# One order per engine, a transposed detour for the modulation, and gates folded into weights in a two-layer adaLN transformer

## What is computed

```python
x = L0_attn_x                                             # (8, 512, 128)
mod = (_silu(L0_c) @ L0_wmod).reshape(8, 6, 1, -1)
sa, ca, ga, sb, cb, gb = (mod[:, k] for k in range(6))
ga = (2 * (ga >= 0) - 1) * jnp.maximum(jnp.abs(ga), 0.25)  # gb the same
h = _layernorm(x) * (1 + ca) + sa
x = x + ga * _L0_attn_ref(h, ...)    # 16 query heads, 4 key heads of 64, rotary, 512 keys
h = _layernorm(x) * (1 + cb) + sb
x = x + gb * _L0_ffn_ref(h, ...)     # FP4-rounded activations and weights, 128 -> 352 -> 128
...                                   # layer 1: the same frame with its own c and wmod
x = x + ga * _L1_attn_ref(h, ...)    # 16 heads of 8; each token attends over the 8 sequences
h = _layernorm(x) * (1 + cb) + sb
x = x + gb * _L1_ffn_ref(h, ...)

def fp4_quant_dequant(x):            # blocks of 16 along the last dimension
    scale = jnp.maximum(jnp.max(jnp.abs(xb), axis=-1, keepdims=True) / 6.0, 1e-12)
    xn = xb / scale                  # |xn| goes to the nearest of 0 .5 1 1.5 2 3 4 6
    return (_GRID[jnp.searchsorted(_MID, jnp.abs(xn))] * jnp.sign(xn) * scale).reshape(shape)
```

## Time and profile before

| | |
|---|---|
| median of 3 runs | 1376.96 us (1372.1 to 1377.42) |
| the profiled execution, its own time | 1373.02 us |
| its span, first to last instruction | 1371.2 us |
| first part (layer 0's attention) | 0 to about 851 us |
| second part (what most of the diff touches) | about 851 to 1371 us |
| mean granted clock of TensorE | 0.899 |

### The profile page before, as it was taken

One profiled execution on the slowest core, in us unless ns is written; L12 is line 12 of the kernel. 1 busy time (PEld: TensorE's weight loads), 2 busy tenths in 40 slices (PEclk: granted clock), 3 DMA queues, 4 the chain that ended last, 5 costly groups with the idle time before them and its releaser, 6 DMA issues. The chain is left out here.

```text
span 1371.2 us, 29825 instructions
## 1 busy us (share of the span) xinstructions
PE 1128.8 (82%) x10832; PEld 711.5 (52%) x10832; DVE 1057.5 (77%) x1468; ACT 625.6 (46%) x1217; POOL 930.0 (68%) x808
## 2 busy tenths in 40 slices
PE   5889999989999989999999996586657776856865
PEld 2245565645655645655655655354335554545654
DVE  4588968868878768779789776677797777789895
ACT  2245645536546446455456452345444343423332
POOL 3379878768788768798798773333578686684331
PEclk9699999999999989999999997688868886887988
DMA  5112112112111111121121120000000000000000
GB/s 151 35 36 59 37 32 60 41 27 56 41 44 41 37 40 47 36 54 43 28 56 43 31 57 21 8 1 1 0 0 0 1 1 1 0 8 9 9 16 23
DMA packets 48627, 42.17 MB, mean 31 GB/s; under 512 B 7869, under 2 KB 46808, under 8 KB 48472
## 3 DMA queue, kind: packets, MB, share of 16 engines
q1 hardware_dynamic: 48040, 39.36, 11.6%
q10 hardware_dynamic: 432, 0.79, 0.2%
HBM read 6.42 MB, written 2.10 MB: 6 GB/s over the span
## 5 line engine op out<-in xcount | busy, mean ns | idle before, releaser
L509 ACT ACTIVATE a_probs<-a_ps_s 128x512 f32<-128x512 f32 x512 | 303.8, 596 | 326.6 <-PE a_ps_s L417 322.4
L742 POOL TENSOR_TENSOR a_p_lo<-a_probs 128x512 f16<-128x512 f32 x384 | 419.0, 1113 | 34.2 <-ACT a_probs L509 31.8
L670 DVE TENSOR_REDUCE a_nmx<-a_ps_m 128x2 f32<-128x1024 f32 x256 | 311.4, 1217 | 34.6 <-PE a_ps_m L400 33.9
L433 PE MATMUL a_ps_o<-a_v_hi,a_probs 128*128 128x65 f16 x2048 | 244.1, 196 | 15.4 <-DVE a_p_lo L677 7.9
L434 PE MATMUL a_ps_o<-a_v_lo,a_probs 128*128 128x64 f16 x2048 | 241.4, 194 | 0.0
L435 PE MATMUL a_ps_o<-a_v_hi,a_p_lo 128*128 128x65 f16 x2048 | 241.1, 195 | 0.0
L433 PEld LDWEIGHTS a_ps_o<-a_v_hi,a_probs 128*128 128x128 bf16 x2048 | 189.9, 99 | 87.9 <-issue 58.9
L415 PE MATMUL a_ps_s<-a_qq,a_kk 128*128 128x512 f16 x512 | 198.0, 387 | 8.2 <-issue 5.3
L434 PEld LDWEIGHTS a_ps_o<-a_v_lo,a_probs 128*128 128x128 bf16 x2048 | 191.8, 99 | 25.1 <-issue 1.5
L417 PE MATMUL a_ps_s<-a_qq,a_k_l 65*128 65x512 f16 x512 | 198.3, 387 | 0.0
L435 PEld LDWEIGHTS a_ps_o<-a_v_hi,a_p_lo 128*128 128x128 f16 x2048 | 191.5, 98 | 0.0
(11 more groups left out here) (234 smaller groups left out, 2108.7 us busy)
## 6 DMA issues: line engine op xcount, KB each, us to landing
a_qq<-a_rhi SPq DMA_DIRECT2D x128, 128.0 KB, 2.4
a_qq<-a_rlo SPq DMA_DIRECT2D x128, 64.0 KB, 2.1
a_kk<-a_rhi SPq DMA_DIRECT2D x64, 64.0 KB, 2.0
a_k_l<-a_rlo SPq DMA_DIRECT2D x32, 64.0 KB, 2.1
out_x<-x_sb SPq DMA_DIRECT2D x8, 256.0 KB, 2.3
a_qq<-a_nmT SPq DMA_DIRECT2D x64, 2.0 KB
a_probs<-in_wq ACTq DMA_DIRECT2D x1, 512.0 KB, 5.1
a_wo<-in_wo SPq DMA_DIRECT2D x1, 512.0 KB, 12.3
```

Of the source, the lines that this page charges most:

```text
L433: nc.tensor.matmul(out, hi, v_hi[:, b % 2, kt, g, 0:65], start=(kt == 0), stop=False)
L509: nc.scalar.activation(probs[:, p % 2, kt, h, :], ps_s[:, i % 2, :], ACT.Exp, scale=DH0 ** -0.5).then_inc(exp_done, 1)
L670: nc.vector.tensor_reduce(nmx[:, p % 2, i:2 * QT:QT], ps_m[:, n % 2, :, :], axis=X, op=ALU.max, negate=True).then_inc(free[n % 2], 1)
L742: nc.gpsimd.tensor_tensor(p_lo[:, p % 2, kt, h, :], pr, pr.bitcast(BF16)[:, 1:2 * L:2], ALU.subtract).then_inc(lo_pool, 1)
```

## The change

1. **Modulation by a detour (`HF`, `HB`).** `HS` no longer multiplies and adds on VectorE. TensorE turns the normalised input (`HF`, four transposes), ScalarE applies scale and shift as per-partition columns while it copies out of PSUM (four activations), TensorE turns it back (`HB`, four transposes), and `HS` reads the result from the PSUM bank, which it holds until it is done.
2. **Gates in weights.** For each FFN, GpSimd makes eight diagonal matrices of the gate (`PD`), and six products of 512 columns (`("P", "wd", f, k, half)`) give down weights for each sequence; two more (`"wo"`) do the same for the output weights. So `Y` is one addition. The output bias goes through the same diagonal matrices (`LY`: a full 128-row fp32 product in place of a 2-row fp16 one). The spread tables, `bc`, `PM8`, `PWO` and three of the four `G` go; `G` now spreads one gate.
3. **Denominator on TensorE (`DS`).** Eight products against the identity sum the probabilities, ScalarE copies, VectorE keeps the reciprocal.
4. **Head layout.** Query and key columns are stored channel-major, `(d h)` and no longer `(h d)`, so `SR` reads with a step of 16 elements.
5. **Order.** `merged_pipeline()` gives way to `merged_order(engine)`, with a table of offsets of its own for each engine and no extra `STEP` between groups 7 and 8.

```diff
-            nc.tensor.matmul(ps_s[0:B, 0, :], cT, wmod[:, 2 * D:6 * D], start=True, stop=True).then_inc(m8_full, 1)
+            nc.tensor.matmul(ps_s[0:B, 0, 0:D], cT, wmod[:, 2 * D:3 * D], start=True, stop=True).then_inc(m8_full, 1)
...
-        if -4 <= s < 0:
-            slots[7].append(("G", s + 4))
+        if s == -1:
+            slots[7].append(("G",))
...
+GROUP_AT = {
+    "PE": {"T1": -131, "GU": (-43, -19, 58, 93), "TD": (396, 407, 423, 426), "HF": -347, "HB": -250},
...
+                if kind == "HF":
+                    n = it[1]
+                    pe.wait_ge(xhat_ok, n + 1)
+                    for t in range(QT):
+                        last = nc.tensor.transpose(bank[:, t * 128:(t + 1) * 128], xhat[:, t, :], ident[:])
+                elif kind == "HB":
+                    n = it[1]
+                    pe.wait_ge(hT_ok, n + 1)
+                    for t in range(QT):
+                        last = nc.tensor.transpose(bank[:, t * 128:(t + 1) * 128], hT[:, t, :], ident[:])
...
+                elif kind == "DS":
+                    r = it[1]
+                    pe.wait_ge(prob_ok, r + 1)
+                    for j in range(B):
+                        last = nc.tensor.matmul(bank[:, 0:B * H1], ident[:], prob[:, :, j, :],
+                                                start=(j == 0), stop=(j == B - 1))
...
+                    elif it[1] == "wd":
+                        f, k, half = it[2:]
+                        pe.wait_ge(diag_ok, 2 * f + 1)
+                        k0, rows = K_TILES[k]
+                        last = nc.tensor.matmul(bank[0:rows, :], ffn_w[f][1][:, k0:k0 + rows], four(diag_f[f], half),
+                                                start=True, stop=True)
...
+                elif kind == "HF":
+                    n = it[1]
+                    if n >= 1:
+                        wait_full(act, ("HB", n - 1))
+                    for t in range(QT):
+                        b = HB * (n % 2) + t
+                        last = nc.scalar.activation(hT[:, t, :], bank[:, t * 128:(t + 1) * 128], ACT.Identity,
+                                                    bias=mod_f[n // B][:, 0, b:b + 1],
+                                                    scale=mod_f[n // B][:, 1, b:b + 1])
+                    last.then_inc(is_free(it), 1)
+                    nc.scalar.drain().then_inc(hT_ok, 1)
...
                 elif kind == "HS":
                     n = it[1]
-                    dve.wait_ge(xhat_ok, n + 1)
-                    if n == B:
-                        dve.wait_ge(bc_ok, B)
-                    nc.vector.tensor_tensor(h[:], xhat[:], gains(n, 2), ALU.mult)
-                    nc.vector.drain()
-                    nc.vector.tensor_tensor(h[:], h[:], gains(n, 1), ALU.add)
-                    nc.vector.drain()
+                    wait_full(dve, ("HB", n))
...
-                    nc.vector.tensor_tensor(yg[:], ps_y[:], gains(n, 3), ALU.mult).then_inc(y_free, 1)
-                    nc.vector.drain()
-                    nc.vector.tensor_tensor(x, x, yg[:], ALU.add).then_inc(x_done, 1)
+                    nc.vector.tensor_tensor(x, ps_y[:], x, ALU.add).then_inc(y_free, 1)
...
-                    nc.vector.tensor_reduce(score[:, t, :, :].rearrange("p s h -> p (s h)"),
-                                            s_prod[:, t % NP, :, :].rearrange("p s (h d) -> p (s h) d", d=DH1),
-                                            axis=X, op=ALU.add).then_inc(s_sum, 1)
+                    nc.vector.tensor_reduce(score[:, t, :, :],
+                                            s_prod[:, t % NP, :, :].rearrange("p s (d h) -> p s h d", h=H1),
+                                            axis=X, op=ALU.add).then_inc(s_red, 1)
```

More of the change, by code:

```diff
@@ new lines, with merged_order, put @@
+PREPARATION_AT = {
[5 rows of a table added]
+    "ACT": ((178, ("P", "cT")), (266, ("P", "qkv")), (306, ("P", "gates")), (645, ("PBH",)), (155, ("PSL",)),
[6 rows of a table added]
+    "POOL": ((141, ("PB",)), (1072, ("PBIAS", 0)), (1036, ("PBIAS", 1)), (975, ("PBIAS", 2)), (637, ("PBL",)),
+            (-623, ("PD", 0)), (401, ("PD", 1)), (476, ("PD", 2))),
+}
+def merged_order(engine):
+    items = []
+    def put(tick, kind, n, at):
+        if isinstance(at, int):
+            items.append((tick + at, len(items), (kind, n)))
+        else:
+            for k, one_at in enumerate(at):
+                items.append((tick + one_at, len(items), (kind, n, k)))
+    for n in range(GROUPS):
+        for kind, at in GROUP_AT[engine].items():
+            put(STEP * n + (GAP if n >= B else 0), kind, n, at)
+    for r in range(ROUNDS1):
+        for kind, at in ROUND_AT[engine].items():
+            put(2 * STEP * r, kind, r, at)
+    for tick, item in PREPARATION_AT[engine]:
+        items.append((tick, len(items), item))
+    return [item for _, _, item in sorted(items)]
@@ L900, in second_part @@
+def second_part(nc, x_sb, modT, mod_f0, gate_bc, ident, ffn_w, dram1, out_x):
+    order = {e: merged_order(e) for e in ("PE", "ACT", "DVE", "POOL")}
     ring, y_job = {}, {}
-    for it in order:
-        if it[0] in ("T1", "TD", "LHT", "KVG", "OT", "P"):
+    for it in order["PE"]:
+        if it[0] in ("T1", "TD", "LHT", "KVG", "OT", "DS", "HF", "HB", "P"):
             ring[it] = len(ring)
@@ L905, in second_part @@
             y_job[(it[0],) + it[1:2] if it[0] == "TD" else it] = len(y_job)
-    prepared = [it for it in order if it[0] == "P"]
+    o_job = {}
+    for it in order["PE"]:
+        if it[0] == "PS" and it[2] % HB == 0:
+            o_job[it[0], it[1], it[2] // HB] = len(o_job)
     with ExitStack() as ex:
@@ L1031, in wait_free, with wait_emptied, four @@
                 eng.wait_ge(free[n % 2], n // 2)
+        def wait_emptied(eng, it):
+            eng.wait_ge(free[ring[it] % 2], ring[it] // 2 + 1)
+        def four(diag, half):
+            return diag[:, half * HB:(half + 1) * HB, :].rearrange("p b d -> p (b d)")
         def is_free(it):
@@ L1573, in item @@
                                               table[:, row:row + 1, :].to_broadcast([128, n, H1]))
-                elif kind == "PWO":
-                    pool.wait_ge(bc_ok, B)
-                    nc.gpsimd.tensor_tensor(wo_g[:], wo_t[:].unsqueeze(1).to_broadcast([D, B, D]),
-                                            mod_bc1[:, :, 0, :], ALU.mult).then_inc(wo_g_ok, 1)
-            for it in order:
+            for it in order["POOL"]:
                 item(it)
```

450 lines of the change are left out of this document (182 added, 268 removed), and 11 rows, old and new, of the table PREPARATION_AT.

## The result

The changed kernel took 1324.83 us, the median of 4 runs (1322.3 to 1325.47), beside 1374.97 us for the kernel before, the median of 4 (1372.1 to 1377.42). The ratio is 0.963, with a 95% interval of 0.961 to 0.966: 50 us faster. The forecast was 1323 us.

The account below looks back on a forecast made before the run. The prediction took VectorE's work plus its hand-over waits to bound the second part. From 1373 us it took 48 there and 4 in the first part, 1321, and forecast 1323 us since the profiled run was under the median; range 1283 to 1364.

Parts of the forecast that it names:

- the second part: The stretch with nearly all of the diff, 521 us long before; forecast at 473 us, 48 less.
- The modulation: In the second part, two VectorE instructions for scale and shift disappear: 42.8 us of VectorE's work go.
- `Y`: At the feed-forward's end, one addition with a PSUM input replaces 24.4 us of VectorE's work: 13.4 us go.
- The denominator: In the softmax, VectorE's row-sum reduction (L1422) goes: 7.5 us less; its 32 products cost PE 8.9 us.
- The score step: VectorE's 32 score sums, reading with a step of 16 elements, cost 21.4 us more; bounds 0 and 21.4.
- the step costs nothing: Rival on the score sums: reading with a step of 16 is free, 21 us better, 1302 us; chance 0.03.
- VectorE's sum: VectorE's busy time in the second part falls from 400.1 to 355 us; the profile should show 350 to 360.
- TensorE's work: PE's busy time in the second part rises from 345.4 to 392 us at the old clock, near 355 if faster.
- The rival in which PE becomes the bound: In the second part, PE's 392 us at its old clock sets the time: 1357 us, range 1345 to 1366; chance 0.20.
- The start: At the second part's start, the first groups wait for gated weights and the detour: +9 us, bounds 4 and 14.
- The orders: In the second part, closing the group gap and filling waits saves 12 us idle; bounds 40 less, 30 more.
- The slower rival: The detour's chain is not hidden in the second part's 16 groups; slower above 3 us a group; chance 0.10.

Follow-up runs that it names:

- e3: The changed kernel with the detour undone: modulation again two VectorE operations, on a constant table, so output differs there; 1358.58 us, ratio 0.990.
- e12: The changed kernel with the feed-forward's end as two VectorE operations again, a product with a table of ones and an addition; 1337.82 us, ratio 0.974.
- e9: The changed kernel with the softmax's row sums back on VectorE and their products and copies removed; 1316.77 us, ratio 0.959.
- e1: The changed kernel with the score step's old head-by-head layout, so VectorE's sums read with unit step; 1298.98 us, ratio 0.947.
- e4: The changed kernel's work in the one merged list of the kernel before, all engines in the same order; 1433.14 us, ratio 1.044.
- e5: The work of the kernel before in the changed kernel's four orders, with the step between groups 7 and 8 closed; 1338.66 us, ratio 0.975.
- e10: The changed work in the one merged list without the detour, modulation as two VectorE operations on a constant table, so output differs; 1391.80 us, ratio 1.014.
- e6: The changed kernel with layer 0's gated down-weight products moved from ahead of group 0 to behind its start; 1320.62 us, ratio 0.961.

## Why the prediction was right, and where only its sum was

The total was right within 2 us and the second part within 2 us (473 forecast, 475.1 measured). The terms behind it were not all right. VectorE's work came out 16 us above the forecast and its idle time 14 us below, and that these two cancel is luck: the total is nearer than the working earns.

- **The modulation** was put at 42.8 us, all of it reaching the end. e3 shows 36 us at the end, of 49.8 us of VectorE's busy time in the new orders. Right in kind, a little large, and not one for one.
- **`Y`** was put at 13.4 us; e12 shows 14 at the end, from 20.9 us of busy time. Right.
- **The denominator** was put at 7.5 us gained, as VectorE's work. e9 shows about 6 us lost (interval 1 to 11). This step failed: I counted the reduction as lying on the path and priced the 32 products and the copies at nothing but PE's busy time. They stand between the exponential and `ON`, where PE, ScalarE and a ring bank are passed one after the other; that this is the cost is my reading, not shown apart. PE's part itself was 12.6 us against 8.9 forecast.
- **The score step** was put at +21.4 us by the row of another reduction with the same step. Measured 1888 ns, as that row (1860 to 1892), and e1 shows 23 us at the end. Right; the case "the step costs nothing" (0.03) is ruled out.
- **VectorE's sum**, 355 us, was measured at 371.1, outside the 350 to 360 that the prediction set as its check. The term that is missing is the waiting for GpSimd inside VectorE's instructions. The prediction saw it in the modulation's means and booked it as leaving with them. In the old list it did leave: e4, the same instructions, has 357.8 us busy, close to the 355. The new orders bring GpSimd's products beside the rounding and add 13 us; e5 against before shows the same, 20 us for the same work. Row by row against before, the large roundings and both forms of L1296 grew by 24 us and the small `N1` rounding shrank by 8, which makes the 16 that are missing.
- **TensorE's work**, 392 us at the old clock (0.79), agrees with e4: 391.7 at 0.81. In the new orders it was 354.0 at 0.87, the prediction's other case. The rival in which PE becomes the bound (0.20) did not come. One of the prediction's own signs of being wrong did: durations of PE changed by more than a tenth in three of its larger groups (down products below, `KVG` 663 to 591 ns, output products L1142 345 to 301, now L1082) and by less in others (gate and up products 532 to 503, sums over the keys 301 to 286). The sum for the time was added up from VectorE's work and waits and did not use PE's durations, so this did not move the forecast. The prediction cited the Trainium skill, "TensorE: Matmul & The Clock Gate", Part 4, for turns that add time and win no clock. The runs do not separate this: with the turns the granted clock rose from 0.83 (e3) to 0.87 (after) in the new orders, where the part also became 34 us shorter, and it stood at 0.82 (e10) and 0.81 (e4) in the one list, where they added 35 us of PE's busy time. The down products, before and after:

```profile
L1177 PE MATMUL s_ps_y<-w_dn,s_h2T 128*128 128x128 f32 x256 | 51.6, 334 | 48.9 <-ACTq L1223 29.8 <-DVE x_sb L1440 19.1
L1126 PE MATMUL s_ps_y<-s_wd_g,s_h2T 128*128 128x128 f32 x256 | 42.7, 291 | 2.7 <-ACTq L1185 2.7
```

- **The start** was put at +9 us. The first `XH` came 9.0 us behind the block's start (3.4 before) and the first reduction of `HS` 14.3 (6.6 before): 5.6 and 7.7 us later, forecast 6 and 9. (Counted to `HS`'s first instruction, which before was the modulation at 5.1, it is 9.2.) The delay is right in size. How much of it reaches the end is open: e6 took 5 us away and gained 3, with some 5 us of uncertainty.
- **The orders** were put at 12 us less idle. This is the term that was most mis-sized. The prediction named the gap and the Silu waits; it did not see the 21.5 us that the score sums waited for GpSimd, which go with the orders (e5, after) and stay with the one list (19.5 in e4). On the old work they give 34 us (e5). On the new work they are worth 111 us (e4), because in the one list the detour's chain is exposed; without the detour the changed work gains 33 us from them (e3 against e10), as the old work does. The prediction added work and order as separate terms; for the detour the two are not separable. The slower rival's point of decision, 3 us a group, was right: in e4 the wait is 71 us over 16 groups, 4.4 us each, and the kernel is slower than before. That groups and rounds overlap, which the prediction held against this rival, did not prevent it: they overlap in the one list too. As I read it, the place of its own that each engine's table gives to each stage did. That is not shown: the four tables and the one list also differ in how well each offset fits, and no run separates the two.
- **The idle total** was forecast at 118 us and measured at 104.0: 14 less, which pays for the 16 us of extra busy time. "The orders fit well" (80 us) was not reached.
- **Banks held by `HS`**: forecast under 30 us of PE's waits; in the changed kernel's groups of PE the idle time ended by that release is 2.2 us before L1029 and 0.6 before L1048. Right.
- **The first part** was put at -4 us. The block starts 6.3 us earlier in the profiled run, and at 845.9 on the mean of all twelve profiled runs with that first part (843.4 to 848.4), 5.8 earlier. The first exponential starts at 54.9 us and not 59.1, 4.2 earlier (forecast 2 to 5). Right, some 2 us small.

The measured parts do not add up to the microsecond. From e5 to the changed kernel 16 us are gained. The parts on their own give 36 + 14 + 6 (the first part) - 23 - 6 - 3 (the start) = 24. The 8 us between are within what four differences with 5 us each can be off, or work that hides behind other work; this stays open.

## What to carry to other kernels

- Moving work off the busiest engine through two others pays only where the order hides the longer chain. Here the same detour gained 36 us with four orders and lost 42 us with one. Test the work in the old order and the old work in the new order before naming the cause.
- Before moving a small reduction to another engine, count what it then waits for. Four reductions of 1.9 us on the busiest engine were at least as cheap as 32 products, 4 copies and a bank each in the middle of a chain (6 us cheaper in one pair of runs and 5 in another, each near its interval).
- Price a layout by the step with which the busiest engine reads. A reduction elsewhere in the same trace gave the price to the last 10 ns before the change was run.
